# Shared gate and up products of a mixture-of-experts layer: the last pass as two products over 64 rows, at partitions 0 and 64

## Chip, cores, metric

The kernel runs on one core of one Trainium2 chip. The metric is the device time of one execution in microseconds, the median of the runs shown. Engines are named as in the profile: PE (matrix products), PEld (its weight loads), DVE, ACT, POOL, and the queues (SPq is the sync engine's DMA queue).

## What is computed

Sixteen images become 197 tokens each (patches times a matrix, a class token, positions), 128 text tokens are put behind them, and two blocks follow on the 325 tokens of 192 values: an attention without softmax, and a mixture of experts with a shared part. The part that the change touches is the shared part, for all T = 16 * 325 = 5200 tokens at once:

```
h = layernorm(h)                            # T x 192
shared = silu(h @ Wsg) * (h @ Wsu) @ Wsd    # Wsg, Wsu: 192 x 928, Wsd: 928 x 192
routed = sum over the chosen experts of w * (silu(g) * u) @ W_down[e],  [g, u] = h @ W_gate_up[e]
return h_in + routed + shared
```

## The kernel before

**Split operands.** A product in the fast 32-bit type keeps fewer bits than a 32-bit value has, so every operand is held as a rounded part (hi) and the remainder (lo), and hi\*hi, hi\*lo and lo\*hi are summed in the same bank. The 192 values of a token stand on partitions: `all_hiA` and `all_loA` hold hi and lo of the first 128, and `all_B` holds both of the last 64, hi on partitions 0 to 63, lo on 64 to 127. The weights' last 64 rows stand twice in `s_hi[:, 1]` and `s_lo[:, 1]`, on both halves. So one tile of gate or up takes five passes (L1194 to L1200): hiA\*s_hi, hiA\*s_lo, loA\*s_hi, B\*s_hi, B\*s_lo. The last pass, with both halves of `all_B` against the weights' lo, also adds the product of two remainders.

**Chunks.** The shared part goes over the tokens in 14 chunks: one of 208 tokens (`PACKED`), then 13 of 384 (`WIDTH`). A chunk has eight up-steps `s_up(o, data, width, m)` (L1186), m = 0 to 7. For m < 7 (FM) a step computes a 128 x 384 tile of gate in one PSUM bank (`sg_ps`) and one of up in another (`su_ps`), 10 products; m = 7 has the remaining 32 columns of both in one bank, 5 products. Gate's last pass increments `sg_mm`, up's last pass `su_mm`.

**What follows a step.** ACT applies silu to the gate bank (`s_silu`, L846, waits for `sg_mm`), DVE multiplies by the up bank (`s_mul`, L1616, waits for silu and for `su_mm`) and increments `s_inter_ready`; ACT and DVE then split the result for the down products (`s_hi_part`, `s_lo_part`). Inside the main loop all steps use the same two banks, so `s_up` of m waits at L1188 until `s_mul` of m - 1 has read them. Where chunks run alone the steps take turns on two pairs of banks and wait for the step before the last.

**The order.** Three chunks (0, 1, 2) run ahead of the loop, mixed with the routing of the experts. Then `together(j)` (L1306) does two experts and one chunk per iteration, written out by hand for each engine; with these inputs some 20 of the 128 experts are chosen at all, so there are 10 iterations, and one chunk of the 14 runs alone at the end. On PE the iteration is:

```
gate_up(j,0,0) s_up 0  gate_up(j,0,1) s_up 1  gate_up(j,0,2) s_up 2  gate_up(j,0,3) s_up 3
turn_rows  count_rows  s_up 4  down  count_rows  down
gate_up(j,1,0) s_up 5  gate_up(j,1,1) s_up 6  gate_up(j,1,2) s_up 7  gate_up(j,1,3)
s_down 0  turn_rows  count_rows  s_down 1  down  count_rows  s_down 2  down
```

`gate_up` (L1155) is ten products 192 wide, `count_rows` (L1138) is one bfloat16 product over 16 partitions (image x counts), `running_counts` (L1081) in the image stage is three bfloat16 products over 128, 128 and 69 partitions. The sync engine's queue loads, per iteration, counts, weights and down weights of two experts, each behind its own wait (L557 to L578).

Of the kernel before, what the change touches and what calls it, by code (L numbers as in the profile page):

```python
# [18 lines left out]
F32 = mybir.dt.float32  # L19
F32R = mybir.dt.float32r  # L20
# [12 lines left out]
DB = D - DA  # L33
# [4 lines left out]
T = B * S  # L38
TL = [128, 128, S - 256]
E = 128  # L40
# [7 lines left out]
FM = IS // 128  # L48
# [5 lines left out]
WIDTH = 384  # L54
TILES = WIDTH // 128
AHEAD = ((0, 208, 2), (208, WIDTH, 3), (208 + WIDTH, WIDTH, 3))
BASE = 208 + 2 * WIDTH
ALONE = 1
PACKED = 2
# [7 lines left out]
AT = 3 * (E + 1)  # L67
# [25 lines left out]
def wait_apart(eng, passed, *waits):  # L93


    for sem, v in waits:
        if not isinstance(v, int) or v > 0:
            eng.wait_ge(sem, v)
            eng.sem_inc(passed, 1)
# [7 lines left out]
def build(nc, xp, txt, wtok, wgu, wdn, wsg, wsu, wsd, w_first, c_base, c_late,  # L107
# [5 lines left out]
    with ExitStack() as ctx:  # L113
# [3 lines left out]
        def sem(name):  # L117
            return ctx.enter_context(nc.semaphore(name))
# [167 lines left out]
        x_rows = [sb(f"x_rows{p}", [CH, 2, YW]) for p in range(2)]  # L286
        w_slot = [sb(f"w_slot{p}", [CH, 2]) for p in range(2)]
        y_rows = sb("y_rows", [CH, 2, D])


        tok_ps, pv_ps, pv2_ps, lg_ps, ct_ps = psum[0], psum[1], psum[2], psum[3], psum[4]
# [117 lines left out]
        put_idx_ready = sem("put_idx_ready")  # L409
        added = sem("added")  # L410

        sg_mm = sem("sg_mm")
        su_mm = sem("su_mm")
        sd_mm = sem("sd_mm")
# [18 lines left out]
        def load_pairs(eng, n_act):  # L433
            return eng.value_load(tables[0:1, bass.ds(n_act, 1)], min_val=K // 2, max_val=E // 2)
# [18 lines left out]
        with nc.Block() as block:  # L453
            @block.sync
            def _(sp):
# [11 lines left out]
                def store_residual(n):  # L467
                    wait_apart(sp, passed, (h1_ready, n + 1))
                    rows = acc[bass.ds(n * S, S), :]
                    sp.dma_start(rows[0:256, :].rearrange("(t p) c -> p t c", p=128), h1[:, 0:2, :]).then_inc(h1_out, 16)  # L470
                    sp.dma_start(rows[256:S, :], h1[0:TL[2], 2, :]).then_inc(h1_out, 16)
# [52 lines left out]
                def step(n, shared=None):  # L524
                    store_residual(n)
                    if not isinstance(n, int) or n < B - 3:
                        load(n + 3)
                    if not isinstance(n, int) or n > 0:
                        store_counts(n - 1)
                    if shared is not None:  # L530
                        load_shared(1, shared)
                    store_normed(n)
                    if not isinstance(n, int) or n > 0:
                        store_weights(n - 1)
# [13 lines left out]
                    step(i)  # L548
                for n in range(B - 3, B - 1):
                    step(n)  # L550
                store_residual(B - 1)
                store_counts(B - 2)
                store_normed(B - 1)
# [3 lines left out]
                def load_counts(j, n, first=False):  # L557
                    if not first:
                        wait_apart(sp, passed, (cnt_mm, 4 * j + 2 * n - 2))
                    e = load_order(sp, 2 * j + n)  # L560
                    sp.dma_start(counts[n % 2][:, :], crow[e, :, :]).then_inc(cr_in[n % 2], 16)
# [10 lines left out]
                def load_down(j, n, first=False):  # L572
                    if not first:
                        wait_apart(sp, passed, (dn_mm, 2 * j + n - 1))
                    e = load_order(sp, 2 * j + n)
                    sp.dma_start(down_w[n % 2][:, :, :],
                                 wdn[e, :, :].rearrange("(c p) n -> p c n", p=F)).then_inc(down_in[n % 2], 16)
# [10 lines left out]
                load_down(0, 1, True)  # L588
                act_n = load_active(sp)
                pairs = load_pairs(sp, act_n)  # L590
                load_counts(0, 2)
                load_counts(0, 3)
                with sp.Fori(0, pairs) as j:
                    for p in range(2):
                        load_counts(j, p + 4)
                        load_weights(j, p + 2)
                        load_down(j, p + 2)
                wait_apart(sp, passed, *[(x, pairs * m + a) for x, m, a in (
                    (raw_in[0], 48, 48), (raw_in[1], 48, 48), (down_in[0], 16, 16), (down_in[1], 16, 16),
                    (cr_in[0], 16, 32), (cr_in[1], 16, 32))])  # L600

                wait_apart(sp, passed, (added, pairs * (PER_PAIR - 16) + ADDED_AHEAD + 16 * BEHIND))

# [393 lines left out]
            def _(pe):  # L997
# [188 lines left out]
                def s_up(o, data, width, m, alone=False, free=None):  # L1186

                    wait_apart(pe, passed, (s_inter_ready, SM * o + m - alone if free is None else free))  # L1188
                    gate_bank, up_bank = up_banks(m, alone)
                    if m < FM:  # L1190
                        products = ((m * 128, 128, gate_bank, sg_mm), (UP + m * 128, 128, up_bank, su_mm))
                    else:
                        products = ((m * 128, 2 * LAST, gate_bank, sg_mm),)
                    for col, r, ps, done in products:  # L1194
                        cols = slice(col, col + r)
                        passes = ((data[0], s_hi[:, 0, cols]), (data[0], s_lo[:, 0, cols]), (data[1], s_hi[:, 0, cols]),
                                  (data[2], s_hi[:, 1, cols]), (data[2], s_lo[:, 1, cols]))
                        for i, (x, w) in enumerate(passes):
                            mm = pe.matmul(ps[0:r, 0:width], w, x, start=i == 0, stop=i == 4)  # L1199
                        mm.then_inc(done, 1)  # L1200
# [621 lines left out]
def constants():  # L1822

    import numpy as np

    i = np.arange(S, dtype=np.float32)
    diff = i[None, :] - i[:, None]
    decay = np.where(diff >= 0, np.float32(0.99) ** np.maximum(diff, 0), 0).astype(np.float32) / np.sqrt(np.float32(D))
    mask = np.zeros((128, SCOLS), np.float32)
    cum = np.zeros((128, 3, SP), np.float32)  # L1830
    for t in range(3):
        o, r = t * 128, TL[t]
        mask[:r, SOFF[t]:SOFF[t] + S - o] = decay[o:o + r, o:]
        cum[:r, t, 1:] = diff[o:o + r, :] >= 0
    p = np.arange(128, dtype=np.float32)
    pairs = (np.arange(E + 1) + 1) // 2
    together = np.minimum(pairs, BEHIND - 1)
    at = np.minimum(np.arange(E // 2), BEHIND - 2) * WIDTH + BASE
    to = np.where(np.arange(E // 2) < BEHIND - 1, at, T + CAP)
    return mask, {  # L1840
        "c_cum": cum,
        "c_up": (p[:, None] < p[None, :]).astype(np.float32),
        "c_ident": np.eye(128, dtype=np.float32),
        "c_iota": np.tile(np.arange(E, dtype=np.float32), (128, 1)),
        "c_ecol": p[:, None].copy(),
        "c_rest": np.tile(ABOVE - np.arange(CAP, dtype=np.float32), (B, 1)),
        "c_rest_col": ABOVE - np.arange(CAP, dtype=np.float32).reshape(2, CH).T,
        "c_tables": np.concatenate([pairs, together, pairs - together, at, to]).astype(np.float32)[None, :],
    }
# [70 lines left out]
```

## Time and profile before

| | |
|---|---|
| median of 3 runs | 731.52 us (730.5 to 732.15) |
| the profiled execution | 730.78 us |
| its span in the profile | 729.1 us |
| mean granted clock of PE | 0.973 |
| PE busy | 678.3 us, 93% of the span |
| DVE / ACT / POOL busy | 471.8 / 331.6 / 211.0 us |
| chain that ended last: PE | 78% |

A row of groups gives a line, an engine, an operation and its tiles, the count, busy time and mean duration, and idle time before it. A row of the timeline gives start and duration. Matrix products are pipelined: one of 384 columns is recorded with 0.34 us, but the next starts long before that has passed, so what a product costs PE is the distance from its start to the next start.

### The profile page before, as it was taken

The page shows a single profiled execution, that of the slowest core. Times are in us where ns is not written, and L with a number is a line of the kernel's source. Part 1 is how long each engine was busy: PE and PEld are TensorE (multiplying, and loading weights), DVE is VectorE, ACT ScalarE, POOL GpSimd, SP SyncE. Part 2 cuts the span into 40 slices and gives each one's busy share as a digit, 9 for nine tenths or more (in the row PEclk, how much of TensorE's full clock was granted, in tenths as well). Part 3 has the DMA queues.
Part 4 walks back from the last instruction along what each step waited for, and adds up shares of the span by engine and source line. Part 5 has one row for each costly group of instructions (what it writes and reads, how often), then busy time and mean ns, then how long its engine had stood idle before and what let it go on. Part 6 is the DMA issues. An engine that isn't in the chain of part 4 may idle for free.

```text
span 729.1 us, 16531 instructions
## 1 busy us (share of the span) xinstructions
PE 678.3 (93%) x4587; PEld 635.9 (87%) x4588; DVE 471.8 (65%) x1486; ACT 331.6 (45%) x802; POOL 211.0 (29%) x310
## 2 busy tenths in 40 slices
PE   4799999999999998799999999999999999999993
PEld 4689998999899887599999999999999999999983
DVE  2247878887888886555667575666666666666641
ACT  1226555555555664244535344444444444444431
POOL 3112323232233200222224242324242424333330
PEclk9689999999999999799999999999999999999997
DMA  7216434544444231513345453545454535353531
GB/s 249 65 56 220 142 108 144 163 146 134 141 140 144 73 110 38 160 31 83 92 91 111 98 111 94 110 94 110 94 110 94 110 94 110 94 110 94 110 58 16
DMA packets 74180, 79.36 MB, mean 109 GB/s; under 512 B 6361, under 2 KB 65897, under 8 KB 74154
## 3 DMA queue, kind: packets, MB, share of 16 engines
q1 hardware_dynamic: 61706, 65.81, 32.2%
q0 software_dynamic: 12160, 12.60, 10.5%
q10 hardware_dynamic: 288, 0.66, 0.3%
q8 instruction: 10, 0.16, 0.1%
q14 instruction: 16, 0.13, 0.1%
HBM read 51.73 MB, written 19.32 MB: 97 GB/s over the span
## 4 chain that ended last, share of the span: by engine, by line
PE 78%; DVE 9%; issue 5%; DMA 3%; ACT 2%; POOL 1%; DVEq 1%; POOLq 0%; ACTq 0%
PE bank L1199 23%; PE bank L1169 10%; PE bank L1011 9%; PE bank L1214 8%; PE bank L1181 7%; PE bank L1003 6%; PE bank L1069 5%; PE bank L1215 3%; PE bank L1041 3%; DVE stats L1357 2%; DMA result<-y_rows,put_idx 2%; DVE h L1381 1%; DVE s_inter L1625 1%; DVE scores L1411 1%; PE bank L1143 1%
## 5 line engine op out<-in xcount | busy, mean ns | idle before, releaser
L1625 DVE TENSOR_TENSOR s_inter<-s_gate,bank 128x384 f32<-128x384 f32 (+1 forms) x112 | 60.4, 540 | 78.1 <-PE bank L1199 65.3
L1214 PE MATMUL bank<-s_dn,s_in_hi 128*128 128x384 f32 (+1 forms) x287 | 88.5, 370 | 3.1 <-DVE s_rows L1640 3.0
L852 ACT ACTIVATE s_gate<-bank 128x384 f32<-128x384 f32 (+1 forms) x112 | 53.5, 478 | 77.2 <-PE bank L1199 77.1
L1199 PE MATMUL bank<-all_hiA,s_hi 128*128 (+4 forms) x210 | 74.1, 353 | 7.3 <-DVE s_inter L1625 4.2
L1011 PE MATMUL bank<-w_tok,patches 128*128 128x192 f32 x384 | 72.6, 343 | 6.9 <-DMA patches<-xp 6.9
L676 POOL DMA_INDIRECT result<-y_rows,put_idx x40 | 64.4, 1610 | 37.9 <-DVE y_rows L1612 16.2
L747 ACT ACTIVATE y<-h,shift,rstd 128x192 f32<-128x192 f32 (+2 forms) x96 | 45.6, 538 | 63.5 <-POOL shift L612 61.7
L1215 PE MATMUL bank<-s_dn,s_in_lo 128*128 128x192 f32 (+1 forms) x287 | 72.6, 253 | 0.0
L1011 PEld LDWEIGHTS bank<-w_tok,patches 128*128 128x128 f32 x384 | 65.9, 201 | 6.5 <-issue 6.5
L1199 PE MATMUL bank<-all_B,s_lo 128*128 (+4 forms) x210 | 71.2, 339 | 0.0
L1199 PE MATMUL bank<-all_B,s_hi 128*128 (+4 forms) x210 | 71.1, 339 | 0.0
L1199 PE MATMUL bank<-all_loA,s_hi 128*128 (+4 forms) x210 | 70.7, 337 | 0.0
L1199 PE MATMUL bank<-all_hiA,s_lo 128*128 (+4 forms) x210 | 70.6, 336 | 0.0
L844 ACT ACTIVATE gate<-bank 116x192 f32<-116x192 f32 x80 | 26.5, 331 | 89.5 <-PE bank L1169 88.1
L1214 PEld LDWEIGHTS bank<-s_dn,s_in_hi 128*128 128x128 f32 (+1 forms) x287 | 54.6, 190 | 7.7 <-DVE s_rows L1640 5.2
L1181 PE MATMUL bank<-down_w,inter 116*96 116x192 f32 x320 | 59.3, 328 | 0.0
L607 POOL TENSOR_SCALAR ve<-mv 128x3 f32<-128x3 f32 x32 | 9.5, 296 | 164.4 <-DVE mv L1361 164.4
L1215 PEld LDWEIGHTS bank<-s_dn,s_in_lo 128*128 128x128 f32 (+1 forms) x287 | 55.3, 193 | 0.0
L1633 DVE TENSOR_TENSOR s_in_lo<-s_inter,s_in_hi 128x384 fp32r<-128x384 f32 (+1 forms) x98 | 52.5, 536 | 0.7 <-ACT s_in_hi L860 0.6
L666 POOL DMA_INDIRECT x_rows<-yw_rows,get_idx x46 | 44.4, 965 | 27.3 <-POOL get_idx L662 20.3
L683 POOL DMA_DIRECT2D result<-s_rows x14 | 19.9, 1418 | 111.6 <-DMA result<-y_rows,put_idx 71.7
L1181 PEld LDWEIGHTS bank<-down_w,inter 116*96 116x96 f32 x320 | 49.7, 163 | 1.7 <-issue 0.2
(201 smaller groups left out, 1853.5 us busy)
## 6 DMA issues: line engine op xcount, KB each, us to landing
raw_gu<-wgu SPq DMA_DIRECT2D x22, 464.0 KB, 5.2
raw_gu<-wgu SPq DMA_DIRECT2D x44, 232.0 KB, 6.0
patches<-xp SPq DMA_DIRECT2D x16, 588.0 KB, 4.4
down_w<-wdn SPq DMA_DIRECT2D x22, 348.0 KB
result<-s_rows POOLq DMA_DIRECT2D x13, 288.0 KB
result<-h SPq DMA_DIRECT2D x16, 192.0 KB
yw_rows<-y SPq DMA_DIRECT2D x16, 192.0 KB
all_hiA<-y_hiA SPq DMA_DIRECT2D x16, 162.5 KB, 2.6
```

The costliest lines, as they stand in the source:

```text
L666: pool.indirect_dma_start(x_rows[p][:, h, :], None, yw[:, :], bass.IndirectOffsetOnAxis(ap=get_idx[p][:, h:h + 1], axis=0)).then_inc(x_in[ ...
L676: pool.indirect_dma_start(acc[:, :], bass.IndirectOffsetOnAxis(ap=put_idx[:, h:h + 1], axis=0), y_rows[:, h, :], None, compute_op=ALU.add) ...
L747: ins = act.activation(c["y"][0:r, t, 0:D], h[0:r, t, :], ACT.Identity, bias=c["shift"][0:r, t:t + 1], scale=c["rstd"][0:r, t:t + 1])
L852: act.activation(s_gate[m % 2][0:r, 0:width], up_banks(m, alone)[0][0:r, 0:width], ACT.Silu).then_inc(s_gate_ready, 1)
L1011: mm = pe.matmul(tok_ps[:, t * D:(t + 1) * D], patches[:, c, t * 128:(t + 1) * 128], w_tok[:, c, :], start=c == 0, stop=c == KC - 1)
L1169: mm = pe.matmul(ps, w, x[:, :], start=i == 0, stop=i == 4)
L1181: mm = pe.matmul(dn_ps[0:CH, h * D:(h + 1) * D], inter[:, m, rows], down_w[n % 2][:, m, :], start=m == 0, stop=m == EM - 1)
L1199: mm = pe.matmul(ps[0:r, 0:width], w, x, start=i == 0, stop=i == 4)
L1214: pe.matmul(bank[0:r, 0:2 * D], s_in_hi[:, m, rows], s_dn[:, m, :], start=m == 0, stop=False)
L1215: pe.matmul(bank[0:r, 0:D], s_in_lo[:, m, rows], s_dn[:, m, 0:D], start=False, stop=False)
L1625: dve.tensor_tensor(s_inter[m % 2][0:r, 0:width], s_gate[m % 2][0:r, 0:width], up, ALU.mult).then_inc(s_inter_ready, 1)
L1633: dve.tensor_tensor(lo_part, s_inter[m % 2][0:r, 0:width], hi_part.bitcast(F32), ALU.subtract).then_inc(s_lo_ready, 1)
```

## The change

Each up-step with m < 7 in a chunk of 384 now does four passes of gate, four of up, and then the fifth pass of both as two products over 64 partitions: gate with the token values' hi on partitions 0 to 63 of `all_B`, up with a copy of them that stands on partitions 64 to 127 of a new buffer `moving_B`. The product of the two remainders is left out there. The two go to different halves of the array's rows (the program marks them as tiles of 64 x 128 at (0, 0) and at (64, 0)) and to different banks. The sync engine copies the 64 x 384 values before each chunk from `all_B` to `moving_B`, behind a wait until the last up product of the chunk before has been done; PE waits for the copy at m = 0. m = 7 and chunk 0 stay as they were.

```diff
+        moving_B = sb("moving_B", [128, WIDTH], F32R)
...
+                def load_moving(at, chunks_done):
+                    wait_apart(sp, passed, (su_mm, FM * chunks_done))
+                    sp.dma_start(moving_B[DB:128, :].bitcast(F32),
+                                 all_B[0:DB, bass.ds(at, WIDTH)].bitcast(F32)).then_inc(moving_in, 16)
+
+                sp.wait_ge(big_out, 48 * 4)
+                load_moving(AHEAD[1][0], 0)
                 store_residual(B - 1)
...
                 pairs = load_pairs(sp, act_n)
+                load_moving(AHEAD[2][0], 2)
                 load_counts(0, 2)
                 load_counts(0, 3)
+                first_k, more_k = load_first(sp, act_n), load_more(sp, act_n)
+                load_moving(BASE, 3)
...
                 with sp.Fori(0, pairs) as j:
                     for p in range(2):
                         load_counts(j, p + 4)
                         load_weights(j, p + 2)
                         load_down(j, p + 2)
+                        if p == 0:
+                            next_moving(j + 1, j + N_AHEAD + 1)
+                with sp.Fori(first_k, BEHIND) as k:
+                    next_moving(k + 1, k + more_k + N_AHEAD + 1)
...
+                    if m < FM and alone != PACKED:
+                        for col, r, ps, done in products:
+                            cols = slice(col, col + r)
+                            passes = ((data[0], s_hi[:, 0, cols]), (data[0], s_lo[:, 0, cols]), (data[1], s_hi[:, 0, cols]),
+                                      (data[2], s_hi[:, 1, cols]))
+                            for i, (x, w) in enumerate(passes):
+                                pe.matmul(ps[:, 0:width], w, x, start=i == 0, stop=False)
+                        if m == 0:
+                            wait_apart(pe, passed, (moving_in, 16 * o))
+                        for part, x, (col, r, ps, done) in ((slice(0, DB), data[2][0:DB, :], products[0]),
+                                                            (slice(DB, 128), moving_B[DB:128, :], products[1])):
+                            pe.matmul(ps[:, 0:width], s_lo[part, 1, col:col + r], x, start=False, stop=True).then_inc(done, 1)
+                        return
```

On PE, in the order of the program, the step m = 6 of the loop (L1199 is the line of a pass; the rows after it are the expert's next products) stood before as:

```order
L1199 MATMUL bank<-all_hiA,s_hi 128x384 [waits s_inter_ready]
L1199 MATMUL bank<-all_hiA,s_lo 128x384
L1199 MATMUL bank<-all_loA,s_hi 128x384
L1199 MATMUL bank<-all_B,s_hi 128x384
L1199 MATMUL bank<-all_B,s_lo 128x384
L1199 MATMUL bank<-all_hiA,s_hi 128x384
L1199 MATMUL bank<-all_hiA,s_lo 128x384
L1199 MATMUL bank<-all_loA,s_hi 128x384
L1199 MATMUL bank<-all_B,s_hi 128x384
L1199 MATMUL bank<-all_B,s_lo 128x384
...
L1169 MATMUL bank<-x_hiA,gu_hi_128 116x192 [waits inter_ready]
```

Gate is complete after the fifth row, up after the tenth. The same step with the change (passes at L1223, the pair at L1228):

```order
L1223 MATMUL bank<-all_hiA,s_hi 128x384 [waits s_inter_ready]
L1223 MATMUL bank<-all_hiA,s_lo 128x384
L1223 MATMUL bank<-all_loA,s_hi 128x384
L1223 MATMUL bank<-all_B,s_hi 128x384
L1223 MATMUL bank<-all_hiA,s_hi 128x384
L1223 MATMUL bank<-all_hiA,s_lo 128x384
L1223 MATMUL bank<-all_loA,s_hi 128x384
L1223 MATMUL bank<-all_B,s_hi 128x384
L1228 MATMUL bank<-all_B,s_lo 128x384
L1228 MATMUL bank<-moving_B,s_lo 128x384
...
L1192 MATMUL bank<-x_hiA,gu_hi_128 116x192 [waits inter_ready]
```

Gate's completion has moved from the fifth place to the ninth, beside up's. In the sync engine's queue, in the loop, the second expert's loads now stand behind the copy (L586 is the first expert's down weights, L571 the second one's counts, L578 its weights):

```order
L586 DMA down_w_121<-wdn 116x4x192
L608 ISA
L608 TENSOR_LOAD tables
L608 ISA x2
L98 ISA
L556 ISA [waits su_mm]
L556 DMA moving_B<-all_B 64x384
L98 REGISTER_ALU
L429 ISA [waits cnt_mm]
...
L578 DMA raw_gu_120<-wgu 128x928
```

The copy and its wait on `su_mm` are new between these two experts' loads.

## Rows read from the trace of the kernel before

**Rows 1.** Windows: the columns are named in the first row.
```profile
core 0: us, PE busy (x) PEld busy (x) DVE busy (x) ACT busy (x) POOL busy (x), PEclk, DMA share, GB/s
371.00:407.00 36.00, 35.56 (x246) 33.79 (x245) 23.71 (x60) 15.96 (x36) 12.46 (x13) 1.00 0.49 103
400.00:700.00 300.00, 294.71 (x2014) 279.86 (x2015) 192.13 (x489) 129.80 (x293) 105.89 (x109) 1.00 0.47 101
```
**Rows 2.** PE's groups in the loop, 335 to 695 us: gate and up passes; counts.
```profile
L1199 PE MATMUL bank<-all_hiA,s_hi 128*128 x140 | 49.6, 354 | 1.4
...
L1143 PE MATMUL bank<-counts,image 16*96 16x326 bf16 x40 | 13.4, 335 | 0.0
```
**Rows 3.** Chain that ended last, inside chunk 2: start us, us, what.
```profile
313.57 3.54 PE bank L1199 x20
```
**Rows 4.** Timeline of PE, steps m = 2 and m = 3: start us, us, what.
```profile
378.13 0.36 PE L1199 MATMUL bank<-all_hiA,s_hi 128*128 x1
...
378.85 0.34 PE L1199 MATMUL bank<-all_B,s_lo 128*128 x1
...
379.73 0.34 PE L1199 MATMUL bank<-all_B,s_lo 128*128 x1
379.91 0.25 PE L1169 MATMUL bank<-x_hiA,gu_hi 128*116 128x192 f32 x1
...
380.91 0.36 PE L1199 MATMUL bank<-all_hiA,s_hi 128*128 x1
```
**Rows 5.** Timeline of ACT, the same stretch.
```profile
378.33 0.33 ACT L844 ACTIVATE gate<-bank 116x192 f32<-116x192 f32 x1 [0.98 <-PE bank L1169]
379.23 0.49 ACT L852 ACTIVATE s_gate<-bank 128x384 f32<-128x384 f32 x1 [0.57 <-PE bank L1199]
```
**Rows 6.** Timeline of DVE, the same stretch.
```profile
378.69 0.35 DVE L1604 TENSOR_TENSOR inter<-gate,bank 116x192 f32<-116x192 f32 x1 [0.34 <-ACT gate L844]
380.11 0.55 DVE L1625 TENSOR_TENSOR s_inter<-s_gate,bank 128x384 f32<-128x384 f32 x1 [1.06 <-PE bank L1199]
382.90 0.55 DVE L1625 TENSOR_TENSOR s_inter<-s_gate,bank 128x384 f32<-128x384 f32 x1 [0.47 <-PE bank L1199]
```
**Rows 7.** Timeline of PE, between step m = 3 and m = 4.
```profile
382.78 0.24 PE L1151 MATMUL bank<-ident,x_rows 96*64 96x96 f32 x1
382.86 0.24 PE L1150 MATMUL bank<-ident,x_rows 96*128 96x96 f32 x1
382.94 0.24 PE L1151 MATMUL bank<-ident,x_rows 96*64 96x96 f32 x1
383.12 0.34 PE L1143 MATMUL bank<-counts,image 16*96 16x326 bf16 x1
383.60 0.41 PE L1199 MATMUL bank<-all_hiA,s_hi 128*128 x1
383.85 0.34 PE L1199 MATMUL bank<-all_hiA,s_lo 128*128 x1
```
**Rows 8.** Timeline of PE in chunk 2, around one product over 16 partitions.
```profile
320.48 0.34 PE L1199 MATMUL bank<-all_B,s_hi 128*128 128x384 f32 x1
320.66 0.34 PE L1199 MATMUL bank<-all_B,s_lo 128*128 128x384 f32 x1
320.93 0.34 PE L1143 MATMUL bank<-counts,image 16*96 16x326 bf16 x1
321.19 0.44 PE L1199 MATMUL bank<-all_hiA,s_hi 128*128 128x384 f32 x1
321.47 0.34 PE L1199 MATMUL bank<-all_hiA,s_lo 128*128 128x384 f32 x1
```
**Rows 9.** Timeline of PEld (weight loads), the same stretch.
```profile
321.19 0.19 PEld L1199 LDWEIGHTS bank<-all_hiA,s_hi 128*128 128x128 f32 x1
321.30 0.19 PEld L1199 LDWEIGHTS bank<-all_hiA,s_lo 128*128 128x128 f32 x1
```
**Rows 10.** Timeline of PE in the image stage: bfloat16 products over 128 partitions.
```profile
107.73 1.14 PE L1011 MATMUL bank<-w_tok,patches 128*128 128x192 f32 x6
108.71 0.42 PE L1086 MATMUL bank<-cum,chosen 128*128 128x326 bf16 x3
108.97 0.51 PE L1058 MATMUL bank<-q_A,yT_A 128*128 128x325 f32 x1
```
**Rows 11.** Timeline of SP's queue, and one group of DMA issues (median us to landing).
```profile
357.35 0.54 SPq L570 DMA_DIRECT2D raw_gu<-wgu  x1
372.49 0.31 SPq L576 DMA_DIRECT2D down_w<-wdn  x1
...
raw_gu<-wgu SPq DMA_DIRECT2D x44, 232.0 KB, 6.0
...
all_hiA<-y_hiA SPq DMA_DIRECT2D x16, 162.5 KB, 2.6
```
**Rows 12.** Chain that ended last, inside chunk 1.
```profile
285.75 5.49 PE bank L1199 x30
291.31 0.56 DVE s_inter L1625
291.87 0.47 DVE s_in_lo L1633
292.34 0.23 DVE reach L1561
292.59 0.42 DVE image L1563
293.05 0.34 PE bank L1143
```

More of the change, by code:

```diff
@@ L410, in build @@
         added = sem("added")
+        moving_in = sem("moving_in")
         sg_mm = sem("sg_mm")
@@ L590, in _, with next_moving @@
                 pairs = load_pairs(sp, act_n)
+                load_moving(AHEAD[2][0], 2)
                 load_counts(0, 2)
                 load_counts(0, 3)
+                first_k, more_k = load_first(sp, act_n), load_more(sp, act_n)
+                load_moving(BASE, 3)
+                def next_moving(i, chunks_done):
+                    at = sp.value_load(tables[0:1, bass.ds(i + AT, 1)], min_val=BASE, max_val=T - WIDTH)
+                    load_moving(at, chunks_done)
                 with sp.Fori(0, pairs) as j:
@@ L600, in _ @@
                     (cr_in[0], 16, 32), (cr_in[1], 16, 32))])
+                wait_apart(sp, passed, (moving_in, pairs * 16 + 16 * (N_AHEAD + 1)))
                 wait_apart(sp, passed, (added, pairs * (PER_PAIR - 16) + ADDED_AHEAD + 16 * BEHIND))
@@ L1837, in constants @@
     together = np.minimum(pairs, BEHIND - 1)
-    at = np.minimum(np.arange(E // 2), BEHIND - 2) * WIDTH + BASE
+    at = np.minimum(np.arange(E // 2), BEHIND - 1) * WIDTH + BASE
     to = np.where(np.arange(E // 2) < BEHIND - 1, at, T + CAP)
```

## The prediction

> **What bounds the kernel now.** I read the windows first: in the main loop an iteration takes 36.00 us and PE has a record running for 35.56 of them, with the granted clock at 1.00, the higher of its two levels, 2.4 GHz [rows 1]. DVE has 23.71 us and ACT 15.96, so it is PE's sequence that sets the end, and what PE gains or loses there counts in full. The groups say that little of PE's time is waiting: the passes that open a gate or up tile sat idle 1.4 us in ten iterations [rows 2]. Next the price of one pass: 20 passes of 384 columns took 3.54 us in the chain [rows 3], 0.177 us from start to start; the recorded 0.34 us is pipeline. Ten passes of an up-step are 1.77 us.
>
> The reader should then look at what lies between two up-steps, since the loop uses one pair of banks. Step m = 2 starts at 378.13 and step m = 3 at 380.91, 2.78 us later; in between stand ten passes (1.78 us) and the ten products of an expert, 379.91 to 380.91 [rows 4]. Gate's last pass ends at 378.85 + 0.34 = 379.19 and silu starts at 379.23 and ends at 379.72 [rows 5]; up's last pass ends at 380.07 and the multiplication starts at 380.11, ends at 380.66 [rows 6], 0.25 us before the next step starts. So silu is now done while up is still being computed, and only the multiplication stands behind the last pass. How fast PE answers it: where the multiplication ended at 383.45 [rows 6] step m = 4 started at 383.60 [rows 7], 0.15 us later, with PE idle before it.
>
> **The change, part by part.**
>
> *The removed pass.* 13 chunks of 384 with 7 steps are 91 steps, 70 of them in the loop. If two products over 64 rows run side by side and nothing else changes, each step loses 0.177 us: 16.1 us in all. That is the most that the change can give.
>
> *The switch of rows.* The trace has no product over 64 rows, but it has one whose array tile is shorter than 128 rows, the counts' product over 16 partitions. In chunk 2 [rows 8] the pass before it holds PE 0.27 us (320.66 to 320.93) in place of 0.177: +0.09, the product before it runs out until 0.07 before its recorded end. The product itself starts at 320.93, and the next one at 321.19, 0.08 before its recorded end, again no overlap. The first pass behind it is recorded with 0.44 us in place of 0.34, and its successor starts 0.28 us later in place of 0.177: its weight load, which otherwise hides beside the product ahead, lies open, +0.10. That this is not the type: bfloat16 products over 128 partitions go in and out without any of it; six passes of 0.162 us from 107.73 end at 108.71, where the first of them starts, and the three with 326 + 198 + 70 columns take 0.26 us, 594 columns at 2.4 GHz being 0.25 [rows 10]. Nor is it the number of columns: products with 64 and with 128 columns follow each other at 0.08 us [rows 7]. So the switch of row tiles costs a drain on the way in, a drain on the way out and an open weight load each time.
>
> The Trainium skill, TensorEngine Tiling (Array Packing), Key Properties, says that a change of the tiling mode drains the engine. For rows the trace agrees (0.27 in place of 0.177 us), for columns it does not (0.08 us per product, no gap). Without that rule and with the pair side by side, the rival A below would be the forecast.
>
> For a step, from the start of the eighth pass: drain +0.09; the first product of the pair with an open load is recorded 0.44; the second ends 0 to 0.11 later (the loads follow each other at 0.11 [rows 9]; I cannot see whether loads to two halves run together); the next product starts 0.07 before that end: 0.37 to 0.48; its own open load +0.10; two passes saved, -0.35. That is **+0.21 to +0.32 us per step** in place of -0.177. Below nothing: if the switch between 128 and 64 rows were free, -0.18. Above: if the second product also waits for the first (0.37 + 0.37), +0.58. I take +0.27, since the only row tile in the trace shows it.
>
> *Gate's completion.* It moves from 0.88 us ahead of up's to beside it, so silu (0.49 us) comes onto the path between two steps. In the loop: passes at 0, then 0.25 (the slot of a first pass after a wait, 383.60 to 383.85 [rows 7]) and six times 0.177: the eighth starts at 1.31. Drain: the pair starts at 1.31 + 0.27 = 1.58, its gate part ends at 2.02, silu runs 2.06 to 2.55, the multiplication, 0.04 later as between 378.66 and 378.69 [rows 5, 6], 2.59 to 3.14, and the next step starts 0.15 later at **3.28** against 2.78. PE's own path would be 2.02 to 2.13, less 0.07, plus 1.00 for the expert's products and 0.10 for the open load: 3.05 to 3.16. So the new chain is the later one, and it hides how well the pair overlaps. Five steps of the loop (1, 2, 3, 6, 7) pay +0.50. Step 4 started 2.69 after step 3 (383.60 - 380.91): +0.59. The pair of step 4 has long work behind it and pays the switch alone, +0.27. Per iteration 2.50 + 0.59 + 0.27 = 3.36, times 10 is **+33.6 us**. DVE and ACT have the room for it (12 and 20 us idle per iteration).
>
> *Outside the loop.* 21 steps (two chunks ahead, the last one), where banks alternate and silu with multiplication (1.04 us) fit beside a step of 1.77: the switch alone, 21 x 0.27 = **+5.7 us**. In chunk 1 a product over 16 partitions waits for a DVE chain that starts with the multiplication behind up's last pass [rows 12]; three times the multiplication now starts some 0.53 later (silu ahead of it): **+1.6 us**.
>
> *The copies.* 14 of 96 KB on SP's queue, 1.4 MB beside 79. One that is larger (162.5 KB) lands in 2.6 us [rows 11]. The copy for the next chunk is issued when up of m = 6 is through, in the iteration from 371 some 23 us in, and the first pair that reads it comes about 13 us later: hidden. Behind its wait stand the second expert's counts and weights. In the iteration before, the weights' last part was issued at 357.35 and the down weights at 372.49 [rows 11]; with the wait that goes to about 360, lands by 366, and is read from 374 on: nothing. If PE gets slower, all of this has more room. The copy adds a wait on PE at m = 0 of each chunk, behind which everything of PE stands, but it is long satisfied.
>
> *Sum.* 33.6 + 5.7 + 1.6 = +40.9 us on the profiled 730.78, 771.7; the median of the runs lies 0.74 above the profiled execution: **772.4 us**, 5.6% slower. Two runs of this kernel differ by up to 0.2%, so less than that cannot be told from no change.
>
> **Rivals.**
>
> *A: the switch is free, the pair runs side by side.* For it: only one kind of short row tile is in the trace, with 16 rows and another type. Against: the control [rows 10]. The chain of silu stays: the pair starts at 1.31 + 0.18 = 1.49, gate ends at 1.83, the next step starts at 3.09: +0.31 five times, +0.40, -0.18 is +1.8 per iteration, +17.7; 21 x -0.177 = -3.7; +1.6. Sum +15.6: 747 us. Chance 0.12. It is to be noted that even this is slower.
>
> *B, faster.* The same, and the wait for the banks does not arise, because silu and multiplication answer in less than the 0.84 us that PE has cover for (380.91 less gate's or up's end at 380.07, without drains); they took 0.04 + 0.49 + 0.04 + 0.55 + 0.15 = 1.26 in the rows, so this needs all of the handover and a part of the work to vanish, or gate to end clearly ahead of up. Then all 91 steps save 0.177: 715 us. The Trainium skill, TensorE: Matmul & The Clock Gate, Part 3, has products on different row groups start about 4 ns apart, and this is the time that such a pair would give by itself. No row here shows it. Chance 0.04.
>
> *C: the two products of the pair do not overlap at all*, each with its drain and load. The gate part still ends at 2.02, but PE's path becomes 2.39 - 0.07 + 1.10 = 3.42, later than the chain: +0.64 five times, +0.59, +0.58 is 4.4 per iteration, 43.7; 21 x 0.58 = 12.2; +1.6. Sum +57.5: 789 us. In this case the change doesn't do what it says. Chance 0.10.
>
> *D: a load comes late.* A copy or the second expert's weights arrive after PE or ACT asks. It decides from a delay of about 8 us on SP's queue, against some 3 expected; each iteration would pay what goes beyond. 775 to 790. Chance 0.03.
>
> *Forecast as worked out*: chance 0.71, own range 761 to 783: down to where the second open load or the drain on the way out costs nothing in the loop's chain, up to a handover that is 0.15 us slower than the one row.
>
> **The numbers.** The likeliest case gives 772. A stands at 747 and must be held, C at 789 may fall out with B: the range is 745 to 786. Faster has only B, 0.04; within 0.2% lies almost no case, 0.02; slower 0.94.
>
> **What would show it.** Right: the pass ahead of the pair holds PE for 0.27 us, the pair's first product is recorded with about 0.44, the product behind it starts about 0.07 before the pair's end and holds PE 0.10 longer than now; PE sits idle 0.1 to 0.2 us ahead of most up-steps in the loop, put down to the multiplication on DVE (L1625 of before), where today there is 1.4 us in all; steps 3.28 us apart; an iteration of 39.4 us; silu starts behind the pair and not 0.9 us before up is done. Wrong: passes around the pair at 0.18 (then A), a second product that starts after the first has ended (then C), PE waiting at m = 0 for the copy or ACT for weights (then D), or steps less than 3.0 us apart, which would break the chain of silu and multiplication that carries most of the sum. A granted clock below 1.00 in the loop would make all of it longer and is not expected, since PE's pauses stay at tenths of a microsecond.

## The result, and the profile after

| | before | changed |
|---|---|---|
| median of 4 runs each | 731.01 us (728.3 to 732.15) | 779.46 us (776.93 to 781.86) |
| ratio | | 1.0663, 95% interval 1.063 to 1.0695 |
| profiled execution | 730.78 us | 776.93 us |
| span | 729.1 us | 775.1 us |
| PE busy | 678.3 us | 705.2 us |

The changed kernel is 6.6% slower; the forecast was 772.4 us, in a range of 745 to 786. The profiled executions differ by 46.2 us, where the sum of the prediction was 40.9. PE has as many products as before (4587 in both profiles), and two of each step now run side by side, yet it is "busy" 27 us longer: products around the switch of rows are recorded longer. In the ten iterations of the loop it is busy 23.7 us longer and idle 17.7 us longer (23.7 us in place of 6.0). Windows over the loop, first of the kernel before, then of the changed one:

```profile
336.52:697.29 360.77, 354.75 (x2432) 336.77 (x2431) 233.85 (x590) 159.53 (x360) 123.24 (x127) 1.00 0.46 99
```
```profile
339.74:741.87 402.13, 378.45 (x2432) 323.55 (x2431) 233.20 (x590) 154.96 (x360) 125.69 (x127) 1.00 0.42 91
```

One iteration of the loop and a longer stretch of it, again in windows (columns as in [rows 1]); an iteration is 40.1 us long in place of 36.0:

```profile
392.60:432.80 40.20, 38.01 (x247) 32.52 (x245) 23.30 (x59) 15.56 (x38) 12.99 (x13) 1.00 0.43 95
400.00:700.00 300.00, 283.82 (x1831) 243.53 (x1830) 174.32 (x442) 116.52 (x271) 97.03 (x98) 1.00 0.43 95
```

In the loop the granted clock is still at 1.00, and DVE and ACT have about as much work as before. PE's first pass of a step in the loop, from the groups by form (352 to 744 us, which leaves out the loop's first steps), answers [rows 2]; the idle time ahead of it was 1.4 us and is now 17.6:

```profile
L1223 PE MATMUL bank<-all_hiA,s_hi 128*128 x135 | 49.9, 370 | 17.6 <-DVE s_inter L1661 16.0 <-DVE y_rows L1648 1.6
```

And the list of who waited for whom names a new wait, that of the multiplication for silu. In the kernel before, the multiplication waited for PE (65.3 us in all) and little for silu (8.6 us). In the changed kernel silu waits for the pair and the multiplication for silu:

```profile
ACT s_gate L875 <- PE bank L1228: 150.4, 89, 5.2
DVE s_inter L1661 <- ACT s_gate L875: 130.8, 99, 3.6
```

PE's timeline over step 2, the answer to [rows 4]:

```profile
507.19 0.41 PE L1223 MATMUL bank<-all_hiA,s_hi 128*128 x1 [0.23 <-DVE s_inter L1661]
507.44 0.34 PE L1223 MATMUL bank<-all_hiA,s_lo 128*128 x1
...
508.49 0.34 PE L1223 MATMUL bank<-all_B,s_hi 128*128 x1
508.76 0.44 PE L1228 MATMUL bank<-all_B,s_lo 64*128 x1
508.76 0.44 PE L1228 MATMUL bank<-moving_B,s_lo 64*128 64x384 f32 x1
509.13 0.35 PE L1192 MATMUL bank<-x_hiA,gu_hi 128*116 128x192 f32 x1
509.31 0.26 PE L1192 MATMUL bank<-x_hiA,gu_lo 128*116 128x192 f32 x1
...
510.62 0.41 PE L1223 MATMUL bank<-all_hiA,s_hi 128*128 x1 [0.22 <-DVE s_inter L1661]
```

Read it from the top. The eighth pass starts 1.30 us into the step and holds PE 0.27 us (508.49 to 508.76), not 0.177: the drain, in which the engine runs out before it changes row tiles. Both products of the pair start at 508.76 and are recorded with 0.44: they run side by side, and their weight loads too:

```profile
508.76 0.18 PEld L1228 LDWEIGHTS bank<-all_B,s_lo 64*128 64x128 f32 x1 [0.25 <-issue]
508.76 0.18 PEld L1228 LDWEIGHTS bank<-moving_B,s_lo 64*128 64x128 f32 x1
509.13 0.18 PEld L1192 LDWEIGHTS bank<-x_hiA,gu_hi 128*116 128x116 f32 x1 [0.19 <-issue]
```

The next product starts at 509.13, 0.07 before the pair's end at 509.20, and holds PE 0.18 in place of 0.09 to 0.10. That it starts so late, with hardly any overlap, is the second drain; that it holds PE longer is the second open load. Then, behind the expert's ten products, PE stands for 0.22 us, and the next step starts 3.43 us after this one; it was 2.78. What it waits for is in the chain of waits of the same stretch:

```profile
507.19 1.64 PE bank L1223 x8
508.83 0.38 PE bank L1228
509.21 0.02 issue
509.23 0.50 ACT s_gate L875
509.73 0.03 issue
509.76 0.04 DVEq L1655
509.80 0.05 issue
509.85 0.02 DVEq L90
509.87 0.04 issue
509.91 0.57 DVE s_inter L1661
510.48 0.14 issue
510.62 0.41 PE bank L1223
```

Passes, pair, silu, multiplication, next step: nothing of this overlaps. Between silu's end (509.72) and the multiplication (509.91) stand 0.19 us with two instructions of DVE's own queue in them; the prediction had 0.04 there.

The steps of one iteration, start to start (from the timelines; 0 to 1, 1 to 2, and so on, the last one from step 7 to the next iteration's step 0):

| | 0 | 1 | 2 | 3 | 4 | 5 | 6 | 7 | sum |
|---|---|---|---|---|---|---|---|---|---|
| before | 2.79 | 2.82 | 2.78 | 2.69 | 5.88 | 2.79 | 2.79 | 13.47 | 36.0 |
| changed | 3.47 | 3.43 | 3.43 | 3.42 | 6.07 | 3.37 | 3.44 | 13.51 | 40.1 |

Step 4, which has long work behind it and so pays the switch alone, costs +0.19. Of the 46.0 us between the spans the loop has 41.4, what lies ahead of it 3.2, the chunk behind it 1.4. The 3.2 is a difference of two things. The first pass of chunk 1 stands at 270.73 us where it was at 272.10, so the stretch ahead of the first changed step came out 1.4 us shorter (its first 45 us with a mean granted clock of 0.85 in place of 0.81). Chunks 1 and 2 together are 4.6 us longer: chunk 2 by 1.5, chunk 1 by 3.0. In chunk 1 the idle time ahead of the counts' products has grown from 5.7 to 7.2 us, and silu stands in the chain of waits there, three times, as forecast. This is the first of them, where [rows 12] had PE's passes right ahead of the multiplication:

```profile
290.13 0.50 ACT s_gate L875
290.66 0.55 DVE s_inter L1661
```

The mean granted clock of chunk 1 was 0.77 in this execution and 0.83 in that of the kernel before, so a part of its 3.0 us may belong to the clock.

### The profile page after: what moved, and what is told of

Read it like the earlier page. It is cut to its first block, busy times and chain, and to the rows that moved or that the text cites. A ratio compares the mean times of both kernels' runs of the same rounds, so it can differ in the third digit from the quotient of the medians.

```text
span 775.1 us, 16661 instructions
## 1 busy us (share of the span) xinstructions
PE 705.2 (91%) x4587; PEld 617.7 (80%) x4588; DVE 471.5 (61%) x1486; ACT 327.0 (42%) x802; POOL 212.8 (27%) x310
## 4 chain that ended last, share of the span: by engine, by line
PE 72%; DVE 13%; ACT 6%; issue 5%; DVEq 1%; DMA 1%; POOL 1%; ACTq 0%; POOLq 0%
PE bank L1223 18%; PE bank L1034 8%; PE bank L1250 8%; PE bank L1204 7%; PE bank L1026 5%; DVE s_inter L1661 5%; PE bank L1092 5%; PE bank L1228 4%; ACT s_gate L875 4%; PE bank L1192 4%; PE bank L1251 3%; PE bank L1064 3%; PE bank L1235 2%; DVE stats L1393 2%; DVE h L1417 1%
## 5 line engine op out<-in xcount | busy, mean ns | idle before, releaser
L1223 PE MATMUL bank<-all_hiA,s_hi 128*128 (+1 forms) x182 | 68.2, 375 | 21.2 <-DVE s_inter L1661 19.5
L699 POOL DMA_INDIRECT result<-y_rows,put_idx x40 | 68.7, 1718 | 62.5 <-DVE y_rows L1648 46.8
L1034 PEld LDWEIGHTS bank<-w_tok,patches 128*128 128x128 f32 x384 | 65.3, 199 | 6.6 <-issue 6.6
L1223 PE MATMUL bank<-all_loA,s_hi 128*128 (+1 forms) x182 | 62.1, 341 | 0.0
L1223 PE MATMUL bank<-all_B,s_hi 128*128 (+1 forms) x182 | 62.0, 341 | 0.0
L1223 PE MATMUL bank<-all_hiA,s_lo 128*128 (+1 forms) x182 | 61.8, 340 | 0.0
L1223 PEld LDWEIGHTS bank<-all_hiA,s_hi 128*128 128x128 f32 x182 | 34.4, 189 | 32.2 <-issue 31.8
L883 ACT ACTIVATE s_in_hi<-s_inter 128x384 fp32r<-128x384 f32 (+1 forms) x98 | 49.4, 504 | 1.3 <-DVE s_inter L1661 1.3
```

The lines of the kernel that those rows point to most:

```text
L699: pool.indirect_dma_start(acc[:, :], bass.IndirectOffsetOnAxis(ap=put_idx[:, h:h + 1], axis=0), y_rows[:, h, :], None, compute_op=ALU.add) ...
L883: act.activation(s_in_hi[:, m, 0:width], s_inter[m % 2][:, 0:width], ACT.Copy).then_inc(s_hi_ready, 1)
L1034: mm = pe.matmul(tok_ps[:, t * D:(t + 1) * D], patches[:, c, t * 128:(t + 1) * 128], w_tok[:, c, :], start=c == 0, stop=c == KC - 1)
L1223: pe.matmul(ps[:, 0:width], w, x, start=i == 0, stop=False)
```

## The experiments

The theory: two terms, the switch of row tiles (drain, open load, drain, open load) and gate's late completion, which puts silu on the path between two steps of the loop. The first rival: the loss is the switch alone, and the wait only shows where PE was made to stand. The second: the pair does not really overlap. The third: the copies on SP's queue have a part in it. Each kernel was timed in three rounds against the kernel before unless told otherwise; the ratios are the comparison, since the chips differ. Beside e1, e2, e3 and e5 the kernel before took 728.93 us.

**e1_late_gate.** The kernel before, gate's fifth pass at the end of the step, all over 128 rows.

```diff
+                    if m < FM and alone != PACKED:
+                        ... four passes of gate, four of up, stop=False ...
+                        for col, r, ps, done in products:
+                            pe.matmul(ps[:, 0:width], s_lo[:, 1, col:col + r], data[2], start=False, stop=True).then_inc(done, 1)
+                        return
```

> All ten passes of a step stay full 128-row passes, no copy and no switch of rows; only gate's fifth pass stands beside up's fifth, at the end of the step. Theory (silu on the path between two steps of the loop is a term of its own): the ninth pass starts 0.25 + 7 x 0.176 = 1.48 us into the step, gate ends at 1.82, silu to 2.35, the multiplication starts 0.19 later as the changed kernel's trace shows, ends at 3.09, and the next step starts at 3.24 in place of 2.79: +0.45 for five steps, +0.56 for step 3 to 4, about +2.8 per iteration, +28 in ten, +1 in chunk 1: about 760 us, and PE idle ahead of most steps of the loop. Rival (the whole loss is the switch of rows, the wait is only what fills it): as before, 731 within 2.

Measured: 761.37 us, ratio 1.0431 (1.0399 to 1.0462). Steps 3.23 us apart, iteration 38.8 us. So the same products in another order cost 32 us, 4.3 points against the change's 6.6; more than half of the change's loss has nothing to do with rows. The rival that put all on the switch falls.

**e2_one_short.** The kernel before, up's last pass over 64 rows.

```diff
+                        last_w, last_x = s_lo[:, 1, cols], data[2]
+                        if m < FM and alone != PACKED and done is su_mm:
+                            last_w, last_x = s_lo[0:DB, 1, cols], data[2][0:DB, :]
```

> The kernel before, with only up's last pass over 64 rows (partitions 0 to 63 of all_B; the product of the remainders is left out for up). Gate's completion stays early. Theory (switch alone): from the measured step 4 of the changed kernel, +0.19 with two passes saved, so one short product per step costs +0.19 + 0.18 = +0.37 us; 91 steps: +34, 765 us, and no new idle of PE ahead of the steps. Rival (entering and leaving a row tile is free, or is paid only once for a kernel): 731.

Measured: 760.76 us, ratio 1.0432 (1.0402 to 1.0461). PE's timeline at step 4:

```profile
507.91 0.34 PE L1202 MATMUL bank<-all_B,s_hi 128*128 x1
508.18 0.44 PE L1202 MATMUL bank<-all_B,s_lo 64*128 x1
508.55 1.54 PE L1181 MATMUL bank<-down_w,inter 116*96 116x192 f32 x8
```

The pass ahead of the product with half the rows holds PE 0.27 us and that product itself 0.37, 0.64 together, where two full ones take 0.35. 31.8 us over 91 steps is 0.35 us per switch there and back, a little under the 0.37 expected; step 4 began with a wait that took part of it (it starts 2.86 after step 3, against 2.69, where the distances to steps 5, 6 and 7 are each 0.37 longer). In the chunk behind the loop, where nothing waits, the steps are 2.14 apart in place of 1.76. No idle time stands ahead of the steps here (the group of first passes shows 0.0):

```profile
L1202 PE MATMUL bank<-all_hiA,s_hi 128*128 (+1 forms) x95 | 33.3, 351 | 0.0
```

**e3_pair_first.** The changed kernel, the pair at the start of the step, gate's and up's four full passes behind it.

```diff
+                            pe.matmul(ps[:, 0:width], s_lo[part, 1, col:col + r], x, start=True, stop=False)
+                        for col, r, ps, done in products:
+                            ... its four passes, start=False, stop on the fourth, which increments done ...
```

> The changed kernel with the pair of 64-row products at the beginning of the step, gate's four full passes and up's four behind it, so gate is complete 0.70 us ahead of up again. Theory (two terms, the switch and silu's place): only the switch is left, 91 x 0.19 = +17 us, 748; steps of the loop 2.98 us apart, hardly any idle of PE ahead of them. Rival (silu's place does not matter, the pair costs what it costs): 777 to 779 as the changed kernel.

Measured: 746.24 us, ratio 1.0229 (1.0205 to 1.0253). Steps 2.97 apart:

```profile
507.58 0.44 PE L1222 MATMUL bank<-all_B,s_lo 64*128 x1
507.59 0.43 PE L1222 MATMUL bank<-moving_B,s_lo 64*128 64x384 f32 x1
507.95 0.44 PE L1228 MATMUL bank<-all_hiA,s_hi 128*128 x1
508.23 0.34 PE L1228 MATMUL bank<-all_hiA,s_lo 128*128 x1
...
510.56 0.44 PE L1222 MATMUL bank<-all_B,s_lo 64*128 x1
```

Same arithmetic, same copies, same switches as the changed kernel, and 4.3 points of the 6.6 are gone. What is left, 17.3 us or 0.19 us per step on average, is the switch less the pass saved: 0.16 in the loop (iterations of 37.1 us in place of 36.0), 0.21 in the chunk behind it (1.97 in place of 1.76). It is still a loss.

**e7_first_same_half.** e3 with both short products on partitions 0 to 63.

```diff
-                                                            (slice(DB, 128), moving_B[DB:128, :], products[1])):
+                                                            (slice(0, DB), data[2][0:DB, :], products[1])):
```

> The kernel with the pair first (e3_pair_first), both products on partitions 0 to 63, one after the other. There PE's own path is the bound, so the overlap must show in full. Theory: 91 x 0.18 = 16 us over e3_pair_first's 746, 762. Rival (the two products do not really overlap, the starts 3 ns apart in the trace are an artefact): 746.

Measured: 761.6 us, ratio 1.0415 (1.0366 to 1.0464), 1.9 points more than e3. The two are now recorded as one stretch of 0.62 us and the next pass starts 0.54 after the first, in place of 0.37:

```profile
510.81 0.62 PE L1222 MATMUL bank<-all_B,s_lo 64*128 x2
511.35 0.44 PE L1228 MATMUL bank<-all_hiA,s_hi 128*128 x1
```

So the overlap of the pair is real and worth its 0.17 us each time.

**e4_same_half.** The same edit on the changed kernel, where the pair stands last.

> The changed kernel, but up's short product is put on partitions 0 to 63 as well (all_B and s_lo there), so the two products of the pair need the same half of the array and cannot run side by side; the result is the same, the copies are still made. Theory (in the loop the path over silu and the multiplication ends after PE's own, so the overlap of the pair is not seen there): each pair takes 0.18 us longer, of 91 only step 4 of each iteration and the 21 steps outside the loop pay it: +5.5 us over the changed kernel, about 785, steps of the loop still 3.43 us apart. Rival (the overlap counts everywhere): 91 x 0.18 = +16, 795.

Measured: 783.57 us, ratio 1.07 (1.0671 to 1.0729), against 1.0663 (1.063 to 1.0695). The steps are 3.43 apart as in the changed kernel, only step 4 is longer (6.23 against 6.07), the iteration 40.3 against 40.1. The two intervals overlap, so the whole times do not tell the 5.5 us expected from nothing; they do rule out the rival's 16. The trace has the rest: in the chunk behind the loop, where the switch alone is paid, the steps are 2.14 apart in place of 1.97. At the other steps of the loop the overlap that the change was built for is not seen at all, since the chain over silu ends later than PE's own path with or without it.

**e5_gate_wait_last.** The changed kernel; DVE waits for silu last.

```diff
-                    dve.wait_ge(s_gate_ready, SM * o + m + 1)
+                    wait(dve, s_lo_ready, SM * o + m - 1)
                     if m < FM:
                         dve.wait_ge(su_mm, FM * o + m + 1)
-                    wait(dve, s_lo_ready, SM * o + m - 1)
+                    dve.wait_ge(s_gate_ready, SM * o + m + 1)
```

> The changed kernel with the three waits ahead of DVE's multiplication in the other order: up's product and the split first, silu last. Theory (the 0.19 us between silu's end and the multiplication are two wait instructions that stand behind the one for silu, since all come true together now): the multiplication starts 0.04 us after silu, 0.15 earlier, the steps of the loop are 3.28 apart in place of 3.43, six per iteration: 9 us less than the changed kernel, 770. Rival (the 0.19 is the time of a signal between ACT and DVE): no change, 777 to 779.

Measured: 769.67 us, ratio 1.0558 (1.0521 to 1.0595), about 8 us less; steps 3.27 apart. Silu and multiplication, from the timelines of ACT and of DVE:

```profile
509.76 0.49 ACT L875 ACTIVATE s_gate<-bank 128x384 f32<-128x384 f32 x1 [1.28 <-PE bank L1228]
...
510.28 0.55 DVE L1660 TENSOR_TENSOR s_inter<-s_gate,bank 128x384 f32<-128x384 f32 x1 [0.60 <-ACT s_gate L875]
```

509.76 + 0.49 = 510.25 and 510.28: 0.03 us, where it was 0.19. The 0.16 between them was not the time of a signal from ACT to DVE, it was the order of three waits.

**e6_one_copy.** The changed kernel with one copy only; from chunk 2 on, up's last pass is taken from chunk 1's values.

> The changed kernel with only the first of the 14 copies into moving_B; the later chunks read that chunk's values, so up's last pass is computed from other tokens. SP's queue has neither the copies nor their waits behind chunk 1. Theory (copies are hidden): as the changed kernel, 779 within 2. Rival (copies or the waits on SP's queue cost something, such as late weights): up to 5 us less, 774.

Measured: 777.46 us, ratio 1.0615 (1.0584 to 1.0645). The intervals of this and of the changed kernel (1.063 to 1.0695) overlap, and the iteration is 40.11 against 40.13 us. So inside the loop the copies cost nothing; if they cost anything outside, it is less than these runs can tell. In the changed kernel's trace, in the timeline of SP's queue, they are issued and landed long before PE asks, and the second expert's weights, now at 409.28 in the queue, come some 10 us after the first expert's down weights without anybody waiting:

```profile
399.68 0.32 SPq L586 DMA_DIRECT2D down_w<-wdn  x1
405.31 0.53 SPq L556 DMA_DIRECT2D moving_B<-all_B  x1
...
409.28 0.54 SPq L580 DMA_DIRECT2D raw_gu<-wgu  x1
```

and by the view of the copies' own line:

```profile
DMA to landing us min/median/max: 2.1/2.4/6.0
```

**e8_counts_128_rows.** If every product in a shorter row tile pays for the switch, the kernel before pays it too, four times per iteration, for the counts. Here `image` and `counts` have 128 partitions, 112 of them zero.

```diff
-        counts = [sb(f"counts{p}", [B, SP], BF16) for p in range(2)]
+        counts = [sb(f"counts{p}", [128, SP], BF16) for p in range(2)]
...
-        image = sb("image", [B, CAP], BF16)
+        image = sb("image", [128, CAP], BF16)
...
+                pool.wait_ge(ct_ready, B)
+                pool.memset(counts[0][:, :], 0.0)
+                pool.memset(counts[1][:, :], 0.0)
+                pool.memset(image[:, :], 0.0).then_inc(rows_zero, 1)
```

(SP's first load and DVE's first image wait for `rows_zero`; loads and DVE still write 16 partitions.)

> The kernel before, where the one kind of product that already paid the switch of rows, counts times image over 16 partitions, is done over 128 partitions, the other 112 being zero (three fills on POOL, once). Theory (the switch is paid by every product in a shorter row tile): each such product costs 0.29 us less of PE's time; of four per iteration two stand ahead of a wait of PE that takes the gain back (0.14 ahead of step 4, 0.30 ahead of the second s_down), two count in full: 10 x 0.58 = 5.8 and some 0.6 in chunk 2: 6 us less than before, 723 to 725. Rival (the price seen around these products is of their waits or their type): 729 to 731 as before, or slower if 128 rows cost more than 16.

Measured: 723.19 us, ratio 0.988 (0.9853 to 0.9907); once more, in five rounds:

> e8_counts_128_rows once more, on the chip of e10_down_order: ratio to before 0.988.

Measured there: 722.9 us, ratio 0.9846 (0.9817 to 0.9874). In the trace of the first of the two the product with 128 rows is cheaper than the one with 16:

```profile
416.32 0.33 PE L1187 MATMUL bank<-down_w,inter 116*96 116x192 f32 x1
416.48 0.30 PE L1149 MATMUL bank<-counts,image 128*96 128x326 bf16 x1
416.62 1.47 PE L1187 MATMUL bank<-down_w,inter 116*96 116x192 f32 x8
```

It holds PE 0.14 us, in [rows 8] 0.26 with 0.09 ahead and 0.10 behind. Iterations of 35.4 us in place of 36.0, 6.2 in ten, as the theory has it. That the ratios say more than 6 us has another part in the profiled execution: the two chunks ahead of the loop are 3.7 us shorter, chunk 2 by the forecast's 0.6 and chunk 1 by 3.1, and in chunk 1 the mean granted clock was 0.91 where it was 0.83 before. Only the 0.6 per iteration is shown to be the switch.

**e9_order and e10_down_order.** In e8 PE waits ahead of step 4 and of the second s_down (by the groups of 400 to 650 us, 1.9 and 3.0 us). e9 moves down products into both waits (both moves below), e10 into the second alone (the second move):

```diff
                     count_rows(j, 3, 0)
+                    down(j, 0, 0)
                     s_up(o, data, WIDTH, 4)
-                    down(j, 0, 0)
                     count_rows(j, 3, 1)
...
                     count_rows(j, 4, 0)
+                    down(j, 1, 0)
                     s_down(o, WIDTH, TILES, 1)
-                    down(j, 1, 0)
                     count_rows(j, 4, 1)
+                    down(j, 1, 1)
                     s_down(o, WIDTH, TILES, 2)
-                    down(j, 1, 1)
```

> On top of e8_counts_128_rows, two moves in PE's order in the loop: the first half of an expert's down products stands ahead of step 4 and ahead of the second s_down (the third s_down goes behind the last down products), so the 0.14 us ahead of step 4 and the 0.30 us ahead of the second s_down, which the shorter counts products have made longer (by 0.29 each), are filled. Theory (these two waits are of PE for DVE and ACT, 0.4 and 0.6 us now): about 1.0 us per iteration, 10 us less than e8_counts_128_rows, 712 to 714. Rival (DVE's order then makes PE wait for the expert's gated product, since its backlog moves by 1.3 us): no gain, 723, or slower.

Measured: 721.67 us, ratio 0.9882 (0.9831 to 0.9932): no gain over e8, as its rival had it. From step 7 to the next step 0 it takes 0.67 us less than e8 (12.48 in place of 13.15), from step 3 to step 7 0.67 more (14.52 in place of 13.85). With the first move step 4 starts 0.7 us later, and PE waits ahead of later steps for the multiplication, 1.21 us here (timeline of PE):

```profile
425.08 0.42 PE L1205 MATMUL bank<-all_hiA,s_hi 128*128 x1 [1.21 <-DVE s_inter L1633]
```

> e9_order without its first move: only the down products of the second expert change places, step 4 stays where it was. Theory (in e9_order the second move took 0.67 us out of the stretch behind step 7, and the first one gave 0.32 back, with PE waiting 0.6 to 1.2 us ahead of step 5 or 6): iterations of 34.7 us in place of 35.4, 6 to 7 us less than e8_counts_128_rows on the same chip, a ratio to before of 0.979. Rival (the end of an iteration only hands its time to the next one's DVE and ACT): as e8_counts_128_rows.

Measured, in five rounds: 718.6 us, ratio **0.9773** (0.974 to 0.9806), beside e8's 0.9846 (0.9817 to 0.9874) on the same chip. Iterations of 34.7 us; no idle time ahead of the s_down products any more:

```profile
L1220 PE MATMUL bank<-s_dn,s_in_hi 128*128 128x384 f32 x155 | 47.8, 370 | 0.0
```

That the first move is what cost e9 its gain follows from this pair. This kernel takes 2.3% less than the kernel before, and it computes the same result.

## Why the prediction held, and where it was off

*What bounds the kernel*: PE's sequence, in both. Each microsecond that a step of the loop got longer is in the time: 10 iterations of 4.1 us are 41 of the 46.

*The switch of rows.* Right in all four parts, from one row of a 16-partition product: drain 0.27 in place of 0.177, product recorded 0.44, next start 0.07 before the end, open load behind it (0.18 in place of 0.10 at the expert's products, 0.28 in place of 0.177 in e3). The two ends were +0.21 (loads to two halves at once) and +0.32 (one behind the other). I took the middle, 0.27; the first end is nearly true, step 4 pays +0.19, the chunk behind the loop 0.21 a step, and e3, which pays nothing else, 17.3 / 91 = 0.19. By the Trainium skill, TensorEngine Tiling (Array Packing), Key Properties, tiles take loads and products in parallel, and the trace agrees: both loads of the pair start at 508.76. Rival C fell with that. It was also priced too high: it gave each product of the pair its own drain and load, 0.74 us for the two, and in e7, with both on one half, they take 0.54.

*Gate's completion.* Right as a mechanism and the largest term: e1 has it alone and costs 32 us. The mis-sized term of the sum is the handover from silu to the multiplication, taken as 0.04 us from a pair of rows of the experts' multiplication (L1604), which has a single wait ahead of it. The shared part's multiplication has three waits ahead of it; silu's is the first of them and here the last to come true, so the two others stand behind it: 0.19. This made the forecast step 3.28 and the real one 3.43, 0.15 x 6 x 10 = 9 us (e1, without any pair, has the 0.19 too). PE accordingly stands 0.22 to 0.33 us ahead of most steps and 0.67 ahead of step 4, where 0.1 to 0.2 was forecast. e5 puts silu's wait last and gets 3.27, the forecast's figure, and 8 us back.

*The sum.* Loop +33.6 forecast, +41.4 measured: +9 for the handover, -0.8 for step 4's pair (0.19 in place of 0.27). Outside +7.3 forecast, and chunks 1, 2 and the last one are 6.0 us longer: 21 steps at 0.21 are 4.4, and chunk 1 has 1.6 beyond its steps, the figure forecast, though at a lower granted clock than before (0.77, 0.83), so the match is not shown to be silu's alone. The spans show 4.6 outside only because the stretch ahead of chunk 1 happened to be 1.4 us shorter. So the miss of 5 us in the sum is +7.8 in the loop, -1.3 outside it and -1.4 of luck.

*Rivals.* A (free switch) falls by the trace. Its remark that even this would be slower is borne out: e1 has no switch at all and is 4.3% slower. B (faster) needed the chain to be shorter than PE's cover and fell by the same rows; what it said of the pair, that both products start together, is in the trace (508.76 and 508.76). D (late loads) falls by e6.

*How the terms add.* e1 costs 4.3 points and e3 costs 2.3; together 6.6, as the change. In the loop a step of e1 is 3.23 us and one of the change 3.43: of the switch only the first drain (0.09) and the pair's open load (0.10) lie ahead of silu and lengthen the chain, while the second drain and load pass inside PE's wait. In e3 all four count and one pass is saved, which happens to give 0.19 as well. So the agreement of the sums is partly one of sizes.

## What to carry to other kernels

Before splitting a product into row tiles, count the way in and out: here 0.37 us there and back beyond the products' own streaming, against 0.18 us that a pair of 384 columns saves. Look also for short row tiles that a kernel has already: here padding a contraction of 16 rows with zero rows to 128 was cheaper than the switch. When passes are reordered, ask which consumer's start moves: the accumulation that is finished first was hiding an engine's work. And where several waits stand ahead of an instruction on a critical chain, put the one that comes true last at the end.

## What the hardware showed that I had not expected

- Loads of weights to two halves of the array's rows start in the same hundredth of a microsecond (508.76 and 508.76), while two loads to the whole array start 0.11 us apart [rows 9].
- A product over 128 partitions costs PE less than the same product over 16: 0.14 us from start to start against 0.26, beside the 0.09 and 0.10 around it.
- Waits that are already true still take their turn on DVE: with two of them behind the wait for silu the multiplication starts 0.19 us after silu's end, and 0.03 us with silu's wait last.
